# A graph layer with attention and routed experts on one core: the combination product of tile 1 later in two layers, the router on unsplit rows, the slot table one step earlier

## The reference, cut to what matters

```python
N, D, H, E, F, TOPK, CAP = 625, 512, 1024, 64, 256, 6, 117
xn = layernorm(x)
for L in range(3):                       # message passing over 20,625 edges
    m = relu(x_[src]) + 1e-7;  e = exp(m * t - max over the edges of dst)
    h = segment_sum(e * m, dst) / segment_sum(e, dst) + x_
    y = relu(ln(h @ w1 + b1)) @ w2 + b2  # w1: 512 x 1024, w2: 1024 x 512
    x_ = y if L == 0 else x_ + relu(ln(y))
    keep x_ as x1, x2, x3
x = x + concat(x1, x2, x3) @ cw + cb + linear_attention(xn)
z = layernorm(x)
logits = z @ router_w.T + bias           # 625 x 64
gates, chosen = top_k(softmax(logits), 6)
shared = sum over 2 of (silu(z @ g.T) * (z @ u.T)) @ d.T / 2
per expert: rows of z that chose it, at most 117, in order of the row number;
            (silu(rows @ w_gate.T) * (rows @ w_up.T)) @ w_down.T, times the gate, added back
out = x + shared + routed
```

## Time and profile before

| | us |
|---|---|
| median of 3 runs | 946.51 (944.45 to 947.73) |
| the profiled execution, its own time | 946.22 |
| its span in the profile | 944.3 |
| PE busy in the span | 874.1 (93%) |
| DVE, ACT, POOL busy | 683.0, 503.3, 387.8 |

### The profile page before, as it was taken

How to read it: one execution, slowest core, us unless ns; L and a number is a source line. 1 busy time by engine, 2 the same in 40 slices (tenths; PEclk the granted TensorE clock), 3 DMA queues, 4 the chain that set the end, 5 groups by cost and what they waited for, 6 DMA issues and landing times. The chain is left out here.

```text
span 944.3 us, 14347 instructions
## 1 busy us (share of the span) xinstructions
PE 874.1 (93%) x4682; PEld 665.9 (71%) x4682; DVE 683.0 (72%) x1150; ACT 503.3 (53%) x875; POOL 387.8 (41%) x341
## 2 busy tenths in 40 slices
PE   4999898899999999899999897999999999999970
PEld 3898798668876788677887775666666666666640
DVE  6966899686446967768678684887767667676665
ACT  2665499746336364364642335565665666656530
POOL 2002101265003831048111446567666676666530
PEclk9999999999999999999999799999999999999985
DMA  6433100342002220114002633899999999999778
GB/s 185 140 122 122 42 1 2 123 133 90 1 30 70 91 90 1 56 45 140 23 12 81 231 128 113 285 328 337 344 329 372 326 336 356 355 346 335 251 190 209
DMA packets 57165, 159.78 MB, mean 169 GB/s; under 512 B 13901, under 2 KB 21651, under 8 KB 48656
## 3 DMA queue, kind: packets, MB, share of 16 engines
q1 hardware_dynamic: 44725, 147.50, 45.8%
q0 software_dynamic: 12288, 11.36, 4.2%
q10 hardware_dynamic: 91, 0.13, 0.1%
HBM read 152.71 MB, written 25.58 MB: 189 GB/s over the span
## 5 line engine op out<-in xcount | busy, mean ns | idle before, releaser
L279 PE MATMUL ps<-split_operands 128*125 128x512 f32 (+4 forms) x540 | 207.2, 384 | 10.8 <-DVE split_operands L1423 4.7
L280 PE MATMUL ps<-split_operands 128*125 128x512 f32 (+4 forms) x540 | 201.4, 373 | 0.0
L281 PE MATMUL ps<-split_operands 128*125 128x512 f32 (+4 forms) x540 | 201.2, 373 | 0.0
L723 POOL DMA_INDIRECT yrow_scratch<-work,row_i x64 | 150.4, 2350 | 100.1 <-ACT work L1079 97.3
L1652 DVE TENSOR_TENSOR gate_up_lo<-expert_weights,split_operands 128x2048 fp32r<-128x2048 f32 x64 | 146.6, 2291 | 10.4 <-ACT split_operands L1061 10.3
L1061 ACT ACTIVATE split_operands<-expert_weights 128x2048 fp32r<-128x2048 f32 x64 | 122.0, 1906 | 10.5 <-DMA expert_weights<-experts_in 10.5
L279 PEld LDWEIGHTS ps<-split_operands 128*125 128x125 f32 (+2 forms) x540 | 101.9, 189 | 33.5 <-DVE split_operands L1423 5.3
L2184 PE MATMUL ps<-expert_weights,work 128*117 128x512 f32 x256 | 121.4, 597 | 0.5 <-issue 0.5
L281 PEld LDWEIGHTS ps<-split_operands 128*125 128x125 f32 (+2 forms) x540 | 102.0, 189 | 19.5
L280 PEld LDWEIGHTS ps<-split_operands 128*125 128x125 f32 (+2 forms) x540 | 102.2, 189 | 16.9
L416 POOL TENSOR_TENSOR split_operands<-work,split_operands 128x512 fp32r<-128x512 f32 x66 | 83.9, 1298 | 56.8 <-ACT split_operands L398 45.3
(11 more groups left out here) (239 smaller groups left out, 1478.8 us busy)
## 6 DMA issues: line engine op xcount, KB each, us to landing
expert_weights<-experts_in SPq DMA_DIRECT2D x64, 1024.0 KB
expert_weights<-experts_in SPq DMA_DIRECT2D x64, 512.0 KB, 11.6
work<-w_in SPq DMA_DIRECT2D x12, 1024.0 KB, 5.1
yrow_scratch<-work SPq DMA_DIRECT2D x5, 1500.0 KB
split_operands<-yrow_scratch SPq DMA_DIRECT2D x4, 1120.0 KB
work<-cw_in SPq DMA_DIRECT2D x3, 1024.0 KB, 5.1
work<-rows_in SPq DMA_DIRECT2D x10, 256.0 KB, 4.7
work<-wmix_in SPq DMA_DIRECT2D x4, 512.0 KB, 5.4
```

Of the source, the lines that this page charges most:

```text
L279: pe.matmul(o, a[1], b[0], start=start, stop=False)
L280: pe.matmul(o, a[0], b[1], start=False, stop=False)
L281: return pe.matmul(o, a[0], b[0], start=False, stop=stop)
L723: pool.indirect_dma_start(yrow, bass.IndirectOffsetOnAxis(ap=row_i[:, e:e + 1], axis=0), OS[e % 4], None, bounds_check=last_row, oob_is_er ...
```

## The change

Five edits, all to orders, waits and buffers; the operations on rows that reach the output keep their precision or, in the router, gain some.

1. In layers 0 and 1 the combination product of tile 1 moves on PE from behind `times_w2(2)` to behind `times_w2(4)` and `x_transpose(3)`; in layer 0 `x_transpose(4)` then stands ahead of `times_cw(2)`, in layer 1 ahead of `times_cw(3)`. Tiles 1 to 4 get other banks (7, 4, 5, 7) and tile 2 another operand buffer, so that of the waits for `cw_add` only that of tile 4 is left behind tile 1. On DVE `cw_add(1)` moves behind the last `message`.
2. At the start of the next layer DVE does `xi_lo(4)` ahead of `zmax_neg`.
3. The router multiplies unsplit rows: `fin_full(t)`, a plain f32 copy on ACT, is added for each tile, and `route(t)` is 4 matmuls instead of 8. `route(2)` moves ahead of `fin_transpose(4)`.
4. Behind layer 2 DVE does the norms first: the third `cw_add` and `fin_norm(2)` come ahead of `choose(1)`, `choose(2)` comes ahead of `fin_lo(3)`, and `split_lo("sd0")` moves from ahead of `choose(1)` to behind `choose(4)`.
5. The slot table is drawn one round earlier; PE transposes it in step 8 and not in step 9; DVE makes `tables` ahead of `shared_lo(8)`; `gate_up_lo(0)` stands ahead of `shared_mul(9)`.

```diff
-CW_BANK = [7, 7, 7, 4, 7]
+CW_BANK = [[7, 7, 4, 5, 7]] * (NL - 1) + [[7, 7, 7, 4, 7]]
...
+            def fin_full(t):
+                if t >= 3:
+                    act.wait_ge(S("router_ps"), t - 2)
+                act.activation(XFULL[XF_BUFFER[t]], ps[:, FT_BANK[t], 0:KD * T].rearrange("p (k n) -> p k n", k=KD),
+                               ACT.Copy).then_inc(S("xf_full"), 1)
...
                 if L:
+                    xi_lo(L - 1, NT - 1)
                     zmax_neg(L)
-                    xi_lo(L - 1, NT - 1)
...
             xi_lo(L, 4)
             cw_add(L, 2)
             fin_stats(2)
-            split_lo("sd0", dve)
+            cw_add(L, 3)
+            fin_norm(2)
+            fin_stats(3)
             choose(1)
-            fin_norm(2)
-            cw_add(L, 3)
-            fin_stats(3)
             cw_add(L, 4)
...
             shared_mul(0)
+            choose(2)
             fin_lo(3)
             fin_lo(4)
-            choose(2)
             choose(3)
             choose(4)
+            split_lo("sd0", dve)
             shared_lo(0)
             shared_mul(1)
             dve.wait_ge(S("key_sb"), 2)
...
+            rounds = iter(range(15))
+            take_eight(next(rounds))
+            for n in range(1, NSH - 2):
+                take_eight(next(rounds))
+                shared_lo(n)
+                take_eight(next(rounds))
+                if n == NSH - 3:
+                    dve.sem_inc(S("table_sb"), 1)
                 shared_mul(n + 1)
             dve.wait_ge(S("table_ps"), 1)
...
+            shared_lo(NSH - 2)
...
             gate_up_lo(0)
+            shared_mul(NSH - 1)
             shared_lo(NSH - 1)
             gate_up_lo(1)
...
                 times_w2(2)
-                times_cw(1)
+                if L == NL - 1:
+                    times_cw(1)
+                    y_transpose(4)
+                    break
                 y_transpose(4)
...
                 times_w2(4)
                 x_transpose(3)
+                times_cw(1)
+                if not L:
+                    x_transpose(4)
                 times_cw(2)
+                if L:
+                    x_transpose(4)
                 times_cw(3)
-                x_transpose(4)
                 times_cw(4)
...
                 for k in range(KD):
-                    for part in range(2):
-                        last = pe.matmul(ps[0:T, RT_BANK[t], 0:E], f(XF[part][:, k, cut(t * T, T)]), RW[:, k, :],
-                                         start=(k == 0 and part == 0), stop=(k == KD - 1 and part == 1))
+                    last = pe.matmul(ps[0:T, RT_BANK[t], 0:E], XFULL[XF_BUFFER[t]][:, k, :], RW[:, k, :],
+                                     start=k == 0, stop=k == KD - 1)
```

More of the change, by code:

```diff
@@ L1035, in _ @@
             fin_hi(1)
+            fin_full(1)
             split_hi("sd0")
@@ L1039, in _ @@
             fin_hi(2)
+            fin_full(2)
             def shared_silu(n):
@@ L1082, in _ @@
             fin_hi(3)
+            fin_full(3)
             fin_hi(4)
+            fin_full(4)
             shared_hi(0)
@@ L1411, in cw_add @@
                 dve.wait_ge(S("cw_ps"), NT * L + t + 1)
[L1412 removed]
+                dve.tensor_tensor(XO[:, t, :], XO[:, t, :], ps[0:T, CW_BANK[L][t], :], ALU.add).then_inc(S("cw_add"), 1)
             def select():
@@ L2141, in _ @@
             fin_transpose(3)
+            route(2)
             fin_transpose(4)
-            route(2)
             shared_transpose(0)
```

49 lines of the change are left out of this document (23 added, 26 removed).

## The result

The changed kernel takes **940.51 us** (median of 6 runs, 937.79 to 941.40) where the kernel before took 947.12 beside it (6 runs, 944.45 to 949.19): ratio 0.9924, 95% interval 0.9906 to 0.9942. I had said 941.2, that is 5.3 less than the 946.5 that I had for the kernel before; against the 947.12 of these runs it is 6.6 less. A second set of 6 runs gave 940.80 (0.9935, 0.9913 to 0.9957). The profiled execution is one of 940.77 with a span of 938.8.

The account below looks back on a forecast made before the run. PE was taken as the bound, so gains come only where it stands or loses work. 1.6 + 2.6 + 1.1 - 1.0 + 0.8 = 5.1 us off 946.22 gives 941.1, stated as 941.2; 8-in-10 range 937.5 to 944.8.

Parts of the forecast that it names:

- End of layer 0: Moved combination product of tile 1 fills PE's 1.39 us idle at the end of layer 0: gain 1.6 us.
- End of layer 1: At the end of layer 1 tile 4's low parts come earlier and the chain moves by 1.9: gain 2.6 us.
- trailing: At layer 1's end PE began `aggregate` 1.5 us behind the first low part it needs; about half was to stay.
- To `shared_transpose(1)`: Behind layer 2, router and norms gain 5.4 us, but the late sd1 load stops PE about 3 us: 1.1 left.
- The extra round: One more 1.74 us table round on DVE ahead of `shared_lo(1)` delays the shared steps: -1.0 us.
- DVE's three rounds would cover the clock: If PE's clock falls in the 3 us stop, `shared_up(2)` is slower, but DVE's three rounds cover it.
- The last shared step: PE's last `shared_down` waits 0.9 us, where PE stood 1.68: +0.8 us.
- A: Slower: sd1's load shares with loads issued behind it, PE stands some 12 us longer, 953.5 us; chance 0.06.
- B: No change: transfers bound the experts, so if their start does not move the end stays at 946; chance 0.08.
- C: No change: the exponentials' chain holds the next layer, so the layers' ends give nothing, 945.3 us; chance 0.10.
- D: Faster: sd1 does not stop ACT, so 5.4 us pass instead of 1.1, giving 936.9 us; chance 0.10.
- 5.4 gained and 4.3 lost by one line: Behind layer 2, 5.4 us gained, given back down to 1.1 by sd0's low part moving behind `choose(4)`, delaying sd1's load.

Follow-up runs that it names:

- memsets late: Changed kernel with POOL's first four memsets moved beside the other four, behind the sd1 split: 939.61 us, ratio 0.9937.
- old table: Changed kernel with table rounds, the table's transpose and the first expert's low part back in their earlier places: 940.98 us, ratio 0.9942.
- router rows only: Kernel before with only the router's rows left unsplit, `route(2)` staying behind `fin_transpose(4)`: 940.46 us, ratio 0.9920.
- sd0 early: Changed kernel with DVE making the low part of sd0 ahead of `choose(3)`, not behind `choose(4)`: 938.28 us, ratio 0.9905.
- all moves: Changed kernel with POOL memsets, `fin_lo(3)`, `shared_lo(0)`, key transposes and sd1's high part reordered, and sd0's low part on POOL: 933.75 us, ratio 0.9857.
- late round: All moves, with the extra table round at the end of the last step that has rounds, not ahead of the first: 930.18 us, ratio 0.9821.
- layers-only run: Kernel before with only the new order at the ends of layers 0 and 1: 943.73 us, ratio 0.9953.
- silu first: Changed kernel with ACT's high part of sd1 behind `shared_out(0)`, not ahead of `shared_silu(1)`: 936.75 us, ratio 0.9893.
- Old norms: Changed kernel with norms, chooses and the sd0 split in the order of before, and `route(2)` behind `fin_transpose(4)`: 938.27 us, ratio 0.9921.

## Why the prediction was right

Term by term, first and second profile of the changed kernel, against before at the same marks:

- **End of layer 0, 1.6:** 1.66 and 1.67. No idle is left, as said.
- **End of layer 1, 2.6:** 2.46 and 2.57. The wait ahead of the last MLP product was to be 1.3 and is 1.08; ahead of `aggregate` 0.76, "under 1". But the 2.5 us are made of two things, and the prediction had one. PE's idle time from M1 to M2 fell from 3.63 to 2.10, that is 1.5. The other 0.9 is clock. Behind the stop of 3.28 the kernel before ran at 1.2 GHz, PE's timeline:
```profile
400.02 0.63 PE L279 MATMUL ps<-split_operands 128*125 128x512 f32 x1
```
The 12 matmuls from 399.18 to 403.63 took 4.45 us, where 12 take 2.8 at 2.4 GHz; after the change the clock is 1.00 there. The "trailing" of 1.5 us, of which I let half stay, was this low clock, and I had not looked at it. Nothing of it stayed: at the start of `aggregate` the gain is 3.2 (106.38 and 103.15 behind M1). By M2 PE, now held by DVE's splits, had given back 0.8. So 2.6 was right by luck in this part.
- **To `shared_transpose(1)`, 1.1:** 1.39 and 2.08. All parts were there: `fin_transpose(2)` 2.4 earlier behind M2 (2.4), `shared_up(1)` 5.1 earlier (5.4), the load of sd1 late, ACT's split waiting for DMA, a stop of 3.37 ("about 3"). Two sizes were off: the load took 4.2 us and not 3.6, and `shared_silu(1)` itself gained only 0.55. The rest of the 1.39 comes from the key transposes and `shared_down(0)`, which PE did behind the start of `shared_silu(1)` before and now does ahead of the stop.
- **The extra round, -1.0:** to S2 the changed kernel lost 1.72 and 1.71, so *this term was sized too small*. DVE's timeline before, `shared_mul(1)` and `shared_mul(2)`:
```profile
538.71 0.42 DVE L1587 TENSOR_TENSOR work<-ps,work 125x256 f32<-125x256 f32 x1 [2.01 <-ACT work L1045]
...
543.70 0.42 DVE L1587 TENSOR_TENSOR work<-ps,work 125x256 f32<-125x256 f32 x1 [0.34 <-DVE work L1593]
```
From the one to the other DVE took 4.99 us and now takes 6.12 (534.53 to 540.65): 1.13, about my 1.0. The other 0.6 is slack that PE had before. S1 came 0.88 us behind the end of `shared_mul(1)` and S2 0.29 behind that of `shared_mul(2)`; after the stop PE follows DVE at once, 0.06 behind at both. I had priced the stop and the round as if they didn't meet. The low clock (0.72 in 534 to 540) adds next to nothing: from S1 to S2 it takes 6.12 us with round and low clock (changed), 6.12 with the round and the clock at 1.00 (memsets late), 6.00 with the low clock and no round (old table), and 4.40 with neither (router rows only). Each of the two is enough for the loss by itself, and I had written that DVE's three rounds would cover the clock: they do. What the round costs by itself depends on how far PE comes behind DVE at S1: with it the step took 5.55 us in sd0 early and 6.75 in all moves, both at 2.4 GHz. The term passed in the sum because the one before it was better by 0.3 and 1.0.
- **The last shared step, +0.8:** 0.65 and 0.75.

The terms make 5.1 by the prediction and 4.4 and 5.4 by the traces. The profiled spans differ by 5.5 and the medians by 6.6; from 4.4 to 5.5 it goes by what none of my terms touches: +0.5, +0.8 and +0.3 behind D (D-H, H-Z, Z-end of the table), and -0.5 for the start, since M0 was 0.5 later. Spreads there are as large as a term, so part of being 0.7 us off is luck.

**The rivals.** A (sd1 shares with the expert loads behind it): the landing was 4.2 us, with a tile's stores and four expert transfers issued behind it before it had landed; far from the 8.7 at which it decides. The Trainium skill ("DMA: Bandwidth & Descriptors", section "Queues, rings and completion order") says that each DMA engine takes its descriptors in ring order; this trace agrees: the earlier transfer is not held up by later ones beyond 0.6 us (4.2 against 3.6). B (experts bound by transfers): H-Z stays 321.4 to 324.0 whenever H comes, and with H 12.8 us earlier (late round, 576.9 against 589.75) the end came earlier by as much (931.5 and 944.3). C: refuted by the layers-only run. D: it didn't happen in the changed kernel, and sd0 early and silu first are that case: 938.3 and 936.8, where D had 936.9.

What the prediction left unsaid is the consequence of its own sum: 5.4 gained and 4.3 lost by one line means that the change had in it a step not worth making. Old norms and sd0 early show it from both sides.

## What to carry to other kernels

When a split, copy or load is moved later to make room, follow the chain that it opens (staging buffer, load queue, landing, the next consumer) and look at what is *queued behind* that consumer, not at when its data are needed: sd1 was needed 24 us later and still stopped PE for 3.4 us. If the wait can't be made shorter, move it behind the urgent work of its engine; here that one line was worth as much as making the load early. When two things hold an engine at one place, taking one away shows nothing: without the extra round or without the low clock the step from S1 to S2 took 6.0 to 6.1 us either way, without both 4.4. And read single edits of 1 to 3 us at marks in the trace, since here the far end of the program varies by as much.

## What the runs showed of the hardware

- DVE's normalisation (`tensor_scalar`, 125x512, f32) takes 0.55 us alone, 1.48 beside a POOL subtraction, and 1.64 and 2.11 beside POOL's memsets in two profiles of one kernel (begun 0.09 behind them each time). MAX8 and MATCH_REPLACE8 beside the other four memsets kept their 0.77. The Trainium skill ("SBUF — State Buffer", section "Who interferes with whom") has this as a port pair that some VectorE instructions, `tensor_scalar` among them, and GpSimd take for whole instructions, and the one that comes second waits. The rows agree for the normalisation (POOL's four memsets took 1.92 us beside the 2.11 and 2.19 beside the 1.64, so more than one of the two may wait), and the price of 0.9 to 1.6 us stood ahead of PE in the kernel before too (1.64 us at 522.86).
- Stops of PE of 3.37, 2.94 and 2.82 us ahead of S1 were each followed by matmuls at 1.2 GHz (0.63 us each instead of 0.39); one of 2.39 with the same work behind it (memsets late) was not, its clock is 1.00 in 532 to 536. Nor was one of 2.84 ahead of `fin_transpose(4)` (old norms), so these lengths alone don't tell. At the end of layer 1 before, a stop of 3.28 was. The low clock costs 1.6 us from S1 to S2 where nothing else holds PE (6.00 in old table, 4.40 without). The Trainium skill says in "TensorE: Matmul & The Clock Gate", section "Why this matters for your kernels", that idle gaps between bursts bring the low clock back; the trace agrees for four of these stops, and the other two show that a gap of this size need not do it.
- At the first expert the same code runs at 1.2 GHz for longer or shorter by the execution: D-H was 11.63 and 12.19 in two profiles of one kernel and up to 13.31 in others. Those 1.7 us are as much as one such edit brings.
